# Attention and expert kernel on one core: projection, transposes, rotation and the split of the maxima moved within a step

## What is computed

```python
q = _apply_rotary(q_emb, split_heads(_proj(layernorm(x), Wq, bq)))   # t * cos + rot(t) * sin
k = _apply_rotary(k_emb, split_heads(_proj(c, Wk, bk)))
v = split_heads(_proj(c, Wv, bv))
p_attn = jax.nn.softmax(einsum('bhtc,bhsc->bhts', q, k) / sqrt(8), axis=-1)
x = x + _proj(p_attn @ v, Wo, bo)
logits = layernorm(x) @ Wr.T + bias            # top 2 of 16, weights renormalized
x = x + routed experts (silu(g) * u @ Wd) + shared expert
```

## Time and profile before

| | us |
|---|---|
| median of 3 runs (760.6 to 761.88) | 761.05 |
| the profiled execution | 760.41 |
| its span in the trace | 758.6 |
| busy PE / PEld / DVE / ACT / POOL | 697.3 / 482.6 / 598.5 / 512.7 / 426.0 |
| from TM of one step to TM of the next, steps 12 to 57 | 8.06 (even step), 7.97 to 8.04 (odd step) |

### The profile page before, as it was taken

One profiled execution on the slowest core, in us unless ns is written; L12 is line 12 of the kernel. 1 busy time (PEld: TensorE's weight loads), 2 busy tenths in 40 slices (PEclk: granted clock), 3 DMA queues, 4 the chain that ended last, 5 costly groups with the idle time before them and its releaser, 6 DMA issues.

```text
span 758.6 us, 19342 instructions
## 1 busy us (share of the span) xinstructions
PE 697.3 (92%) x5941; PEld 482.6 (64%) x5941; DVE 598.5 (79%) x1597; ACT 512.7 (68%) x1211; POOL 426.0 (56%) x755
## 2 busy tenths in 40 slices
PE   2698999999999999999999999999897999999995
PEld 1355565666666666666666666666565978888784
DVE  6888999899899889989998998998645544466666
ACT  4267787888888888888888888887751155554441
POOL 3554656645756667666666566664344025655562
PEclk9999999999999999999999999999999999999998
DMA  5665543444465455544444444444073535678774
GB/s 170 175 174 161 156 124 107 124 134 145 141 176 156 150 164 147 155 131 138 142 143 152 146 121 149 137 140 153 32 225 116 165 92 162 221 244 279 230 236 151
DMA packets 97147, 118.81 MB, mean 157 GB/s; under 512 B 12821, under 2 KB 81304, under 8 KB 97049
## 3 DMA queue, kind: packets, MB, share of 16 engines
q1 hardware_dynamic: 89684, 100.16, 44.0%
q0 software_dynamic: 6864, 16.93, 6.4%
q10 hardware_dynamic: 500, 0.49, 0.3%
HBM read 76.87 MB, written 42.11 MB: 157 GB/s over the span
## 4 chain that ended last, share of the span: by engine, by line
PE 69%; DVE 12%; POOL 8%; issue 7%; DMA 2%; ACT 1%; another core or an unknown queue 0%; SPq 0%; ACTq 0%; DVEq 0%; POOLq 0%
PE bank_o L1376 13%; PE bank_s L1402 11%; PE bank_st L1439 10%; PE bank_st L1559 9%; DVE M L1157 5%; PE bank_s L1577 4%; PE bank_st L1354 4%; PE bank_b L1420 2%; POOL work L739 2%; POOL parts_sb L742 2%; POOL work L744 2%; PE bank_b L1446 2%; PE bank_a L1494 2%; PE bank_b L1485 2%; PE bank_s L1361 2%
## 5 line engine op out<-in xcount | busy, mean ns | idle before, releaser
L1157 DVE TENSOR_REDUCE M<-bank_s 128x2 f32<-128x512 f32 x512 | 339.3, 682 | 49.4 <-PE bank_s L1402 41.5
L826 ACT ACTIVATE Pr<-bank_st 128x512 f32<-128x512 f32 x503 | 292.6, 598 | 64.0 <-PE bank_st L1439 53.3
L1402 PE MATMUL bank_s<-QK 72*128 72x256 bf16 x1024 | 202.0, 280 | 8.8 <-DMA QK<-parts 5.9
L1439 PE MATMUL bank_st<-QK 98*128 98x256 bf16 x1006 | 195.8, 276 | 0.9 <-ACT Pr L826 0.2
L1376 PE MATMUL bank_o<-Pr,wide 128*32 128x256 f32 x2048 | 140.3, 390 | 0.5 <-ACT Pr L826 0.5
L1402 PEld LDWEIGHTS bank_s<-QK 72*128 72x128 bf16 x1024 | 91.0, 99 | 68.8 <-DVE M L1157 30.6
L739 POOL TENSOR_TENSOR work<-work 128x256 f32<-128x256 f32 x62 | 45.0, 725 | 158.5 <-DVE work L1215 158.5
L766 POOL DMA_INDIRECT results<-Pr,ids_out x79 | 78.5, 994 | 80.4 <-issue 45.7
L1439 PEld LDWEIGHTS bank_st<-QK 98*128 98x128 bf16 x1006 | 90.4, 98 | 45.9 <-ACT Pr L826 18.7
L1559 PE MATMUL bank_st<-QK,xn 128*128 x316 | 82.3, 383 | 1.0 <-issue 1.0
L1376 PEld LDWEIGHTS bank_o<-Pr,wide 128*32 128x32 f32 x2048 | 56.3, 110 | 36.0 <-issue 15.0
(11 more groups left out here) (175 smaller groups left out, 1061.2 us busy)
## 6 DMA issues: line engine op xcount, KB each, us to landing
QK<-parts SPq DMA_DIRECT2D x127, 288.0 KB
parts<-parts_sb SPq DMA_DIRECT2D x64, 192.0 KB, 2.4
wide<-slots SPq DMA_DIRECT2D x79, 130.0 KB
ctx_kv<-ctx_dram SPq DMA_DIRECT2D x64, 128.0 KB, 2.4
xT_all<-results SPq DMA_DIRECT2D x14, 512.0 KB
QK<-w_gu SPq DMA_DIRECT2D x8, 512.0 KB
parts<-parts_sb SPq DMA_DIRECT2D x31, 128.0 KB, 2.9
X<-x_dram SPq DMA_DIRECT2D x7, 512.0 KB, 5.4
```

The source lines that it names most:

```text
L826: nc.scalar.activation(Pr[k][:], bank_of_scores(at.r, k)[:], ACT.Exp, scale=SCALE).then_inc(s_exp, 1)
L1157: nc.vector.tensor_reduce(M[:, c, 2 * ORDER[k]:2 * ORDER[k] + 2], bank_s[S_BANK[c][k]][:].rearrange("p (a s) -> p a s", a=2), AX.X, ALU.ma ...
L1402: last = nc.tensor.matmul(bank_s[S_BANK[at.mod(2)][k]][:, T * t:T * t + T], Q[c][0:KR, ORDER[k], P * t:P * t + P], K[c][0:KR, ORDER[k], :] ...
L1439: last = nc.tensor.matmul(bank_of_scores(at.r, k)[:, T * s:T * s + T], K[c][0:MROW + 2, ORDER[k], P * s:P * s + P], Q[c][0:MROW + 2, ORDER ...
```

## The change

The arithmetic and the number of instructions stay as they are; only places move.

- PE: the projection goes from behind S 4 to ahead of S 3. BT goes from k 6 to k 7 of the even step, behind S 7 and ST 7. xt goes from k 7 of the odd step to k 0 of the even step behind it, behind ST 0.
- ACT: both halves of the turned copy stand ahead of E 3 (before: ahead of E 4 and of E 5).
- DVE: the rotation goes from behind R 5 and `On` to behind R 4; `On` stays behind R 5. `LG` goes from behind R 2 to behind R 1.
- POOL: the split of the maxima goes ahead of `rest`, the third operation of the parts.

```diff
-        SWAP_APART = 1
+        SWAP_APART = 0
...
                     nc.gpsimd.tensor_tensor(parts[:, p, h, 0, :], rc[:, h], rs[:, h], ALU.add).then_inc(s_p1, 1)
-                    wait(pool, s_p1, at.value(1, 7))
-                    nc.gpsimd.tensor_tensor(rest[:, h], qk[:, h], parts[:, p, h, 0, :], ALU.subtract).then_inc(s_r1, 1)
                 if at.has(2) and at.r != -2:
                     split_maxima(at)
                 if at.has(6) and at.r >= -4:
+                    wait(pool, s_p1, at.value(1, 7))
+                    nc.gpsimd.tensor_tensor(rest[:, h], qk[:, h], parts[:, p, h, 0, :], ALU.subtract).then_inc(s_r1, 1)
...
-                        if k == 4 + SWAP_APART * half and at.has(6):
+                        if k == 3 + SWAP_APART * half and at.has(6):
                             swap(at, half)
...
-                    if k == (3 if at.r == DRAIN else 2) and at.r % 2 == 0 and at.has(-6):
+                    if k == (3 if at.r == DRAIN else 1) and at.r % 2 == 0 and at.has(-6):
...
-                    if k == 5 and at.has(6):
+                    if k == 4 and at.has(6):
...
-                    if k == 4 and at.has(6):
+                    if k == 3 and at.has(6):
...
+                    if even and k == 0 and at.has(-6):
+                        wait(pe, s_xs, at.pairs(-6, add=1))
+                        held(at, bank_b, (s_rope, at.value(1, 6), NB))
...
-                    if even and k == 6 and at.has(-2):
+                    if even and k == 7 and at.has(-2):
...
-                    if not even and k == 7 and at.has(-5):
-                        wait(pe, s_xs, at.pairs(-5, add=1))
-                        held(at, bank_b, (s_rope, at.value(1, 7), NB))
```

More of the change, by code:

```diff
@@ L1183, in step @@
                                                 br[:], ALU.add).then_inc(s_lge, 1)
+                    if k == 4 and at.has(6):
+                        h = at.mod(2)
+                        wait(dve, s_turn, at.value(2, 14))
+                        wait(dve, s_p1, at.value(1, 5))
+                        if at.r == -6:
+                            dve.wait_ge(s_bias, 1)
+                            nc.vector.tensor_copy(bias_qk[:], bank_o[:, 2:6]).then_inc(s_bias, 1)
+                            dve.wait_ge(s_bias, 2)
+                        bank = bank_a if at.r == -5 else bank_b
+                        nc.vector.scalar_tensor_tensor(rc[:, h, :], bank[:, 0:T], bias_qk[:, 2 * h:2 * h + 1],
+                                                       tab[:, 0, :], ALU.add, ALU.mult)
+                        nc.vector.scalar_tensor_tensor(rs[:, h, :], turned[:], bias_qk[:, 2 * h + 1:2 * h + 2],
+                                                       tab[:, 1, :], ALU.add, ALU.mult).then_inc(s_rope, 1)
                     if k == 5 and at.has(-1):
@@ L1426, in step @@
                                              start=True, stop=True).then_inc(s_bias, 1)
+                    if at.has(2):
+                        c = at.mod(4, 2)
+                        if k == 0:
+                            v = 32 * ((at.r + 2) // 4 + 1)
+                            wait(pe, s_stk[c], v if at.i is None else 32 * at.i + v)
+                        wait(pe, s_red, at.value(8, 16 + k + 1 - S_BACK[at.mod(2)][k]))
+                        for t in range(2):
+                            last = nc.tensor.matmul(bank_s[S_BANK[at.mod(2)][k]][:, T * t:T * t + T],
+                                                    Q[c][0:KR, ORDER[k], P * t:P * t + P], K[c][0:KR, ORDER[k], :],
+                                                    start=True, stop=True)
+                        last.then_inc(s_S, 1)
                     if at.has(0):
@@ L1442, in step @@
                         last.then_inc(s_ST, 1)
+                    if even and k == 0 and at.has(-6):
+                        wait(pe, s_xs, at.pairs(-6, add=1))
+                        held(at, bank_b, (s_rope, at.value(1, 6), NB))
+                        for c in range(2):
+                            last = nc.tensor.transpose(bank_b[:, P * c:P * c + P],
+                                                       ring[:, at.pair(-6) % RING, P * c:P * c + P], ident[:])
+                        last.then_inc(s_xt, 1)
                     if not even and k == 1 and at.has(-3):
@@ L1496, in step @@
                         last.then_inc(s_vp, 1)
-                    if not even and k == 7 and at.has(-5):
-                        wait(pe, s_xs, at.pairs(-5, add=1))
-                        held(at, bank_b, (s_rope, at.value(1, 7), NB))
-                        if at.i is None:
-                            wait(pe, s_x2, at.pairs(-3, add=1), NP)
-                        for c in range(2):
-                            last = nc.tensor.transpose(bank_b[:, P * c:P * c + P],
-                                                       ring[:, at.pair(-5) % RING, P * c:P * c + P], ident[:])
-                        last.then_inc(s_xt, 1)
                     g = PLACED.index((at.r, k)) if (at.r, k) in PLACED else -1
```

## The result

The changed kernel takes 774.04 us (median of 4 runs, 772.42 to 778.4), the kernel before 761.0 beside it: 1.0179 of it, 95% interval 1.0136 to 1.0222. The profiled execution takes 773.41 (span 771.6) against 760.41. The forecast was 763.5, with 753 to 769 as its range: the direction was the likelier one, the size is wrong by 10.5 us.

What follows compares the result with a forecast made beforehand. PE looked like the bound, with waits; after the change DVE would end most odd halves. Pairs of steps 12 to 57 +2.5, early steps +.2, start-up -.5, last steps +.7: +2.9 on 760.41, 763.3, put at 763.5; range 753 to 769.

Steps and rivals of the forecast that it cites:

- the kind with the positions' matmuls: Odd half, one of four, with .5 of positions' matmuls on PE; forecast 8.1, with PE (7.6 plus additions) later than DVE.
- D: Label for the odd half that holds the positions' matmuls; forecast at 8.1.
- P: Start of the projection behind TM in odd halves: 1.07 in two kinds, about 1.2 and 1.53 in the others, average 1.22.
- A: The plain odd half, with no routing operation ahead of X; forecast at 7.94.
- C: The odd half where X came latest in the kernel before; forecast at 8.40.
- B: The odd half with routing operations at (0,6) to (1,1); forecast at 8.37, with .30 for one between R 6 and R 7.
- slower than forecast: Rival, odd halves: X late in every kind, P 1.5 in three, a pair .25 above forecast, 769; chance .11.
- The even half: Even half, TM to TM: waits of .34 and .15 removed, .34 and .05 added, 8.06 to 7.96, a gain of .10.
- The split: Split of the maxima on POOL: claimed to no longer end the odd half, ready .4 ahead of TM.
- Start-up and ends: Outside steps 12 to 57: start-up -.5 (clock up to 1.6 more), steps up to 10 +.2, last steps +.7.
- Both halves gain: Rival, steps 12 to 57: R 7 does not hold S 2, a pair gains .3, 753; chance .27.
- the two cancel: Rival, steps 12 to 57: odd half loses .1, a pair changes by 0, 758.5 to 762.5; chance .22.

Runs made afterwards that it cites:

- e1: The changed kernel with the positions' matmuls of groups 0 to 5 one place later, at k 7 behind S 7 and ST 7; ratio 1.0146 to the kernel before.
- e10: The changed kernel with the positions' matmuls in the free half of bank_o, ahead of the values' product, without waiting for On; ratio 1.0107 to the kernel before.
- e7: The changed kernel with four routing operations moved earlier, out of the stretch where POOL works; ratio 1.0115 to the kernel before.
- e12: The changed kernel with both the diffs of e7 and e10; ratio 1.0051 to the kernel before.
- e2: The kernel before with only the POOL part of the change, the split of the maxima ahead of rest; 754.2 us, ratio 0.9888 to the kernel before.
- e6: The changed kernel without its POOL part, the subtraction of the rest again ahead of the split of the maxima; ratio 1.0293 to the kernel before.
- e5: The kernel before with the POOL part, BT and xt moved as in the change; projection, copies, rotation and LG as before; ratio 0.9781 to the kernel before.
- e9: The changed kernel with the positions' matmuls in bank_b at k 5, waiting for the rotation, and their readers on DVE later; ratio 1.0323 to the kernel before.

## Why the prediction failed

- **The step that failed** is "8.1 in the kind with the positions' matmuls, where PE is later than DVE". It measured 9.25, six times: 6.8 of the 8.9 us by which the 23 pairs miss the forecast (11.4 for 2.5), and the whole misses it by 10. I laid PE's *work* in this kind over the changed order, but not the wait of that work: I moved `On` back to 5.05 and further in odd halves, and asked only what BT waits for. The positions' matmuls wait for `On` too, through `bank_a`, and S 7 and R 7 queue behind them. e1 (they start .10 behind `On` wherever they stand) and e10 (-.71 without the wait) show it. .27 of D's 1.14 is the next point (e7); with both gone (e12) D is 8.23, .13 above the forecast.
- **P was mis-sized, 1.07, 1.2, 1.53 and 1.07.** It measured 1.07, 1.59, 1.51 and 1.37. The rule was right: in all kinds the projection stands .10 behind `X`, and TM in A and C at P + 6.84, in B .13 more (forecast: P + 6.87, and .30 more in B). But `X` at .80 to 1.02 behind TM in three kinds is the condition of my rival "slower than forecast", though by another cause than the late R 6 that it names: the routing operations ahead of `X` in B and D are lengthened beside POOL's work (L1037 .59 for .21, L1050 .50 for .17). e7 shows this as the cause. I took their times from the kernel before, where these two happened to begin just behind POOL's L744 and took .23 and .18; the one ahead of C was lengthened there already (.42), so C came out right. In the old order the POOL part of the change alone brings this on (e2: `X` at .90 for .63 in B, .72 for .50 in D). In the new order it isn't the POOL part: without it (e6) `X` is no earlier, because the work that POOL does behind the split then lies beside the same operations. The .30 that I took for one routing operation in the earlier trace rows was itself such a lengthened one: .37 there, .21 in the changed kernel. In B the two errors nearly cancel (8.37 forecast, 8.56 measured).
- **The even half** was forecast at 7.96 and is 8.00, for the reasons given: BT free, ST 5 late by .34. e5 against the changed kernel (7.79, 8.00) shows what this exchange costs.
- **The split** no longer ends the odd half: right, and it is ready .9 ahead of TM, not .4. e2 shows its worth alone, -7.7, which I had put into one sum with the loss. Of the change, the POOL part brings 8 us, BT and xt on top of it another 8, and projection, copies, rotation and `LG` at their new places lose 27 (the last TM of e5 at 526.12, of the changed kernel at 553.41). In the 23 pairs alone these are 4.2, 5.0 and 20.6; of the 8, some 1.2, and of the 27, .8 lie in the half at step 59, which goes with the chip.
- **Start-up and ends**: -.5 was -.3, and that it is so near is luck: the clock's lower level went as I left open, the halves from the TMs of steps 1 and 2 give 1.6 back, and those of steps -1 and 0, where I forecast nothing, lose 1.2. The early steps cost +1.3 for +.2. The last steps cost +.6 for +.7, also by another way: -.6 up to the last TM and +1.2 behind it, where PE's clock was at the lower level for some us.
- **Both halves gain, and the two cancel**, fall: S 2 does wait for R 7 in odd halves, and a pair grows by .46, not by .11.

What stays open: D keeps .27 behind A in e2 too; whether that is the wait for the last reader, as in e10, wasn't tried. Nor were the early and the last steps taken apart by a run, nor projection, copies, rotation and `LG` tried one by one.

## What to carry to other kernels

When an operation is moved later, list everything that waits for its result, the rare ones too: a product that stands in one step of eight, on an engine that works in order, delays all that is queued behind it. A change of four parts should be costed part by part, also against leaving each out: here two parts bring 16 us and the rest loses 27. An operation's duration in the old trace may already hold a wait beside a neighbour: compare the same line's durations over the trace. And when an engine's work is shifted in time, ask which short operations of its neighbour it now lies beside.

## What the hardware showed

An operation of VectorE on two SBUF inputs that begins while one of GpSimd's tensor operations of .67 or more runs ends with it, .03 to .09 behind its end: in the changed kernel 6 of 6 L1037 (.59 for .21), 6 L1041 (.51), 11 L1050 (.50 for .17) in the repeating steps, in e6 up to .72. The kernel before has it too (12 L1041 of .36 to .43, 6 L1046 of .45). Reduces, and operations with one input in PSUM (`X`, `On`, L1055), keep their time beside the same work. The Trainium skill ("SBUF — State Buffer", the section on the two separate sides) says so: a VectorE operation with two SBUF inputs and a GpSimd operation that reads SBUF share a port pair, and the one that starts later is blocked for the whole of the other. The trace agrees for VectorE as the later one.

The chip itself moved the time by 1.8% (762 to 748 for the same kernel), nearly all of it in the stretch behind the steps (217 to 221 against 205 to 208), while the halves of steps 12 to 57 agree to .02. And the granted clock doesn't follow from one wait alone: of six idle stretches of 1.19 us on PE (e9) five were followed by a granted clock of .50 and one by 1.00; none of the six of .74 in the changed kernel was.
